# Inverse roots by a power instruction, the last fold stage on TensorE, and a new instruction order in a gated state-space and FFN kernel

## The reference, cut to what matters

```python
xc  = causal_conv4(in_proj_w @ ctx) + conv_b;  u = silu(xc)          # 256 channels
dt, Bm, Cm = split(x_proj_w @ u);  delta = softplus(dt_proj_w @ dt + dt_proj_b)
state = state * exp(delta * A) + (delta * u) * Bm;  y = sum_n(state * Cm)   # A = -exp(A_log)
y = swapaxes((y + D * u) * silu(layernorm(x)), 1, 2)      # layernorm(x) stands as (channel, token) here
x2 = x + tanh(g_xattn) * y
t  = act_quant(layernorm(x2))                  # per token: round(x * 128 / absmax)
h  = silu(t @ Wg_ternary) * (t @ Wu_ternary)
h  = act_quant(fwht(h))                        # Walsh-Hadamard over 1024
out = x2 + tanh(g_ffn) * (h @ Wd_ternary)
```

## Time and profile before

| | |
|---|---|
| three runs | 218.87, 219.84, 220.48 us, median 219.84 |
| profiled execution | 220.84 us, of which the span of instructions is 218.4 |
| busy | PE 195.1, DVE 185.9, ACT 170.4, POOL 106.7 us |
| first scan starts | 32.47 us |
| last `times_C` ends | 181.15 us |
| last instruction on DVE | 215.70 us |

### The profile page before, as it was taken

How to read it: one execution, slowest core, us unless ns; L and a number is a source line. 1 busy time by engine, 2 the same in 40 slices (tenths; PEclk the granted TensorE clock), 3 DMA queues, 4 the chain that set the end, 5 groups by cost and what they waited for, 6 DMA issues and landing times.

```text
span 218.4 us, 3808 instructions
## 1 busy us (share of the span) xinstructions
PE 195.1 (89%) x1296; PEld 160.7 (74%) x1296; DVE 185.9 (85%) x290; ACT 170.4 (78%) x298; POOL 106.7 (49%) x143
## 2 busy tenths in 40 slices
PE   2849997999999999999999999999899997669883
PEld 1638985898797888868889797888687676534761
DVE  1860709899989999999999999999999996879983
ACT  1357989999899998779997988899877812794473
POOL 1003080269805347935999992299940399600000
PEclk9967999999999999999999999999999999996998
DMA  5895000000000000000000000000000000000001
GB/s 139 236 358 193 3 2 2 0 0 3 0 0 3 0 0 6 0 0 0 5 0 0 3 0 0 27 2 24 3 0 0 2 27 24 0 0 3 24 24 48
DMA packets 8147, 6.33 MB, mean 29 GB/s; under 512 B 2202, under 2 KB 7874, under 8 KB 8130
## 3 DMA queue, kind: packets, MB, share of 16 engines
q1 hardware_dynamic: 6610, 6.01, 8.4%
q10 hardware_dynamic: 1520, 0.10, 0.5%
HBM read 5.05 MB, written 1.05 MB: 28 GB/s over the span
## 4 chain that ended last, share of the span: by engine, by line
PE 41%; POOL 7%; ACT 6%; DVE 5%; issue 2%; DVEq 0%; POOLq 0%; ACTq 0%
PE PY L477 8%; PE UP L414 7%; PE BC L414 6%; PE GP L596 5%; POOL wnat L1529 3%; POOL wnat L1530 3%; PE GP L627 2%; PE GP L611 2%; PE BC L461 2%; PE UP L649 1%; PE UP L668 1%; ACT ctxs L1200 1%; DVE state L1642 1%; DVE wnat L1828 1%; ACT wq L1239 1%
## 5 line engine op out<-in xcount | busy, mean ns | idle before, releaser
L1067 ACT ACTIVATE decay<-delta,zero_c,aneg 128x255 f32<-128x255 f32 x128 | 65.8, 590 | 0.2
L1642 DVE TENSOR_TENSOR_SCAN state<-decay,BC 128x512 f32<-128x512 f32 x32 | 38.8, 1212 | 8.3 <-ACT decay L1067 6.3
L1642 DVE TENSOR_TENSOR_SCAN state<-decay,UP 128x512 f32<-128x512 f32 x32 | 38.5, 1204 | 0.4 <-issue 0.2
L1725 DVE TENSOR_TENSOR prod<-state,BC 128x1024 f32<-128x1024 f32 x32 | 38.4, 1199 | 0.5 <-PE BC L461 0.5
L414 PE MATMUL BC<-diagB,duT 128*128 128x256 f32 x128 | 33.9, 387 | 1.0 <-DVE state L1642 1.0
L414 PE MATMUL UP<-diagB,duT 128*128 128x256 f32 x128 | 33.5, 385 | 1.1 <-DVE state L1642 1.1
L1529 POOL TENSOR_TENSOR wnat<-wnat 128x512 f32<-128x512 f32 x18 | 22.9, 1273 | 22.4 <-DVE wnat L1769 21.5
L477 PE MATMUL PY<-id,prod 128*128 128x128 f32 x256 | 32.8, 273 | 0.1
L477 PEld LDWEIGHTS PY<-id,prod 128*128 128x128 f32 x256 | 29.1, 141 | 2.3 <-DVE prod L1725 0.3
L1463 POOL TENSOR_SCALAR_AFFINE_SELECT diagB<-BT 128x1024 f32<-128x1024 f32 x16 | 17.3, 1090 | 22.1 <-ACT BT L1078 15.4
L414 PEld LDWEIGHTS UP<-diagB,duT 128*128 128x128 f32 x128 | 22.9, 190 | 6.2 <-issue 3.3
(11 more groups left out here) (254 smaller groups left out, 392.5 us busy)
## 6 DMA issues: line engine op xcount, KB each, us to landing
xs<-in_x_dram SPq DMA_DIRECT2D x1, 1024.0 KB, 8.6
wnat<-in_L_ffn_w_gate_dram SPq DMA_DIRECT2D x1, 1024.0 KB, 11.9
wnat<-in_L_ffn_w_up_dram SPq DMA_DIRECT2D x1, 1024.0 KB, 13.9
wnat<-in_L_ffn_w_down_dram SPq DMA_DIRECT2D x1, 1024.0 KB, 12.7
out_dram<-ot SPq DMA_DIRECT2D x8, 128.0 KB, 1.7
ctxs<-in_ctx_dram SPq DMA_DIRECT2D x1, 384.0 KB, 4.2
ctxs<-in_ctx_dram SPq DMA_DIRECT2D x1, 128.0 KB, 2.7
inw<-n_L_xattn_in_proj_w_dram SPq DMA_DIRECT2D x1, 128.0 KB, 2.8
```

What stands on the lines that cost most here:

```text
L1067: last = nc.scalar.activation(decay[:, m % RING, h, n, 1:L], delta[:, b % 2, h, 1:L], ACT.Exp, bias=zero_c[:], scale=aneg[:, h, NB * j + n ...
L1642: nc.vector.tensor_tensor_scan(state[:, g % STATES, h].rearrange("p n l -> p (n l)"), decay[:, g % RING, h].rearrange("p n l -> p (n l)"), ...
L1725: nc.vector.tensor_tensor(prod[:, g % RING].rearrange("p h n l -> p h (n l)"), state[:, g % STATES].rearrange("p h n l -> p h (n l)"), PC. ...
```

## The change

1. **Roots.** The first norm's inverse roots come from POOL: `first_rstd` there computes -mean, var + eps, (var + eps) ** -0.5 by a `tensor_tensor` with `ALU.pow` over 128x8, and the product. It stands ahead of `diagonals(0,0)`. ACT's Ln and Exp and DVE's four small instructions and two copies go. `second_rstd(f)` on POOL has one add, one power (128x2) and two small products, in place of ACT's `rstd2` and eight small POOL instructions. `last_rstd(c)` on POOL (add, power, product, 128x1) replaces ACT's Ln and Exp and DVE's `last_second_rstd(c)`; both calls stand after POOL's last `fold_tile(2,1,2)`.
2. **Table loads.** With no Ln and Exp in the tail, one `for_exp` and one `for_silu` go: `decays(31,*)` now come ahead of the Silu of batch 2, and the Silu set stays to the end.
3. **Last fold stage on PE.** `last_fold(t)` has two stages. The third is done by `last_inter_T` in PSUM: for each pair of blocks (a, a+1) it transposes a and accumulates the transpose of a+1, or a product with the negated identity (`nid`, made by POOL's `negate_id`). The halves hold other blocks (`last_block`).
4. **Loads.** The two gates move from ACT's queue to SP's, behind the Hadamard matrix and ahead of D; `alog` has its own semaphore and is issued earlier; `dtb` is issued ahead of x. `tanh_gates` moves behind the first `for_silu` after `decays(1,0)`; `gate_out(0)` waits for it.
5. **Order.** All four lists are rearranged.

```diff
+            def first_rstd():                                   # POOL
+                pool.wait_ge(dve_stat1, 1)
+                link_first.begin(pool, 0)
+                nc.gpsimd.tensor_scalar(nm1[:], mv1[:, :, 0], -1.0, 1.0, ALU.mult, ALU.mult)
+                link_first(nc.gpsimd.tensor_scalar(ve1[:], mv1[:, :, 1], LN_EPS, 0.0, ALU.add, ALU.add))
+                link_first(nc.gpsimd.tensor_tensor(r1[:], ve1[:], mhalf[:], ALU.pow))
+                nc.gpsimd.tensor_tensor(mr1[:], nm1[:], r1[:], ALU.mult).then_inc(pool_r1, 1)
             def second_rstd(f):
...
+                link(nc.gpsimd.tensor_scalar(ve2[:], mv2[:, :, 1], LN_EPS, 0.0, ALU.add, ALU.add))
+                link(nc.gpsimd.tensor_tensor(rn2[:], ve2[:], mhalf[:, 0:LC], ALU.pow))
                 for c in range(LC):
...
+            def last_rstd(c):
+                link = last_r_link[c].begin(pool, 0)
+                pool.wait_ge(last_stat, c + 1)
+                pool.wait_ge(act_xn, B - 1)
+                col = slice(c, c + 1)
+                link(nc.gpsimd.tensor_scalar(ve2[:, col], mv2[:, c, 1:2], LN_EPS, 0.0, ALU.add, ALU.add))
+                link(nc.gpsimd.tensor_tensor(rn2[:, col], ve2[:, col], mhalf[:, col], ALU.pow))
+                nc.gpsimd.tensor_scalar(mr2[:, col], mv2[:, c, 0:1], rn2[:, col], -1.0, ALU.mult, ALU.mult).then_inc(last_rn, 1)
...
             def last_inter_T(t, i):
-                pe.wait_ge(last_folded, 4 * t + 3 + i)
+                pe.wait_ge(last_folded, 3 * t + 2 + i)
...
-                for j in range(NI // 2):
-                    a = 2 * j + i
-                    last = nc.tensor.transpose(last_half(GP, i)[:, P * j:P * (j + 1)], fold[:, t, P * a:P * (a + 1)], id32[:])
+                for g in range(2):
+                    for k in range(2):
+                        dst = last_half(GP, i)[:, P * (2 * g + k):P * (2 * g + k + 1)]
+                        a = last_block(i, 2 * g)
+                        one, other = (inter[:, t, P * b:P * (b + 1)] for b in (a, a + 1))
+                        nc.tensor.matmul(dst, one, id32[:], is_transpose=True, start=True, stop=False)
+                        if k == 0:
+                            last = nc.tensor.matmul(dst, other, id32[:], is_transpose=True, start=False, stop=True)
+                        else:
+                            last = nc.tensor.matmul(dst, other, nid[:], start=False, stop=True)
...
+            for i, g in enumerate((g_xattn, g_ffn)):            # SP, after had, before dskip
+                sp.dma_start(gates[:, i:i + 1], g.partition_broadcast(P)).then_inc(ld_gate, 16)
```

More of the change, by code:

```diff
@@ L171, in gated_ssm_ffn @@
         bank6, bank7 = UP[:, 0:512], UP[:, 512:1024]
-        mean1, ve1, nt1 = (UP[:, 8 * i:8 * (i + 1)] for i in range(3))
         wgT = wT[:, 0].rearrange("p (h i) -> p h i", h=HALF)
@@ L814, in _ @@
             C_rows(7)
+            accumulate(4)
             drive_rows(9, 0)
-            accumulate(6)
-            weight_T(1)
-            drive_rows(9, 1)
-            C_rows(8)
-            weight_T(2)
-            dt_proj(2)
+            weight_T(2)
+            accumulate(5)
+            drive_rows(9, 1)
+            dt_proj(2)
+            C_rows(8)
+            accumulate(6)
+            drive_rows(10, 0)
             accumulate(7)
-            drive_rows(10, 0)
+            gate_T(1)
@@ L850, in _ @@
             C_rows(13)
             drive_rows(15, 0)
-            gate(0, 1)
+            up(0, 1)
             drive_rows(15, 1)
+            accumulate(11)
+            C_rows(14)
             accumulate(12)
-            C_rows(14)
-            up(0, 0)
             drive_rows(16, 0)
+            C_rows(15)
             drive_rows(16, 1)
-            C_rows(15)
             accumulate(13)
-            x_dbl(3)
             drive_rows(17, 0)
+            dt_proj(3)
             drive_rows(17, 1)
+            inter_T(0, 0)
@@ L888, in _ @@
-            hadamard_mm(0, 1)
-            down(0, 0)
-            accumulate(18)
-            tokens_T(1)
             drive_rows(22, 0)
-            drive_rows(22, 1)
-            accumulate(19)
+            du_T(3)
             gate(1, 0)
             C_rows(21)
+            drive_rows(22, 1)
+            gate(1, 1)
             drive_rows(23, 0)
-            du_T(3)
-            gate(1, 1)
+            gate_T(3)
+            q2_T(0, 1)
+            up(1, 0)
             drive_rows(23, 1)
+            drive_rows(24, 0)
@@ L901, in _ @@
+            C_rows(22)
+            down(0, 1)
             accumulate(20)
[L902 to L904 removed]
             drive_rows(24, 1)
[L906 to L908 removed]
             C_rows(23)
@@ L1033, in exp_A @@
                 act.wait_ge(consts, 1)
-                act.wait_ge(ld_gate, 16 * 3)
-                nc.scalar.activation(aneg[:], alog[:], ACT.Exp, bias=zero_c[:]).then_inc(act_gate, 1)
+                act.wait_ge(ld_A, 16)
+                nc.scalar.activation(aneg[:], alog[:], ACT.Exp, bias=zero_c[:]).then_inc(act_A, 1)
             def inw_out():
@@ L1211, in q2_out_early @@
                                ).then_inc(act_q2T, 1)
-            def last_rstd(c):
-                link = last_r_link[c].begin(act, 0)
-                act.wait_ge(last_stat, c + 1)
-                link(nc.scalar.activation(ln2[:, c:c + 1], mv2[:, c, 1:2], ACT.Ln, bias=eps_c[:]))
-                nc.scalar.activation(r2[:, c:c + 1], ln2[:, c:c + 1], ACT.Exp, bias=zero_c[:], scale=-0.5).then_inc(last_r, 1)
-                link.end()
             def last_norm(c):
@@ L1294, in _ @@
             for_exp()
+            dt_rows(1)
+            decays(1, 1)
+            copy_BT(1)
             decays(2, 0)
             decays(2, 1)
-            dt_rows(1)
-            copy_BT(1)
+            high_pieces(1)
             decays(3, 0)
-            high_pieces(1)
             decays(3, 1)
@@ L1303, in _ @@
             decays(4, 0)
+            softplus(1)
             decays(4, 1)
-            softplus(1)
-            gate_out(0)
             decays(5, 0)
             decays(5, 1)
+            gate_out(0)
+            weight_abs(1)
             weight_abs(2)
@@ L1823, in last_fold @@
                 dve.wait_ge(last_mul, 2 * (t + 1))
-                for i in range(FOLDS):
+                for i in range(FOLDS - 1):
                     src, dst = ((inter, fold), (fold, inter))[i % 2]
@@ L1922, in _ @@
             scan(0, 0)
-            first_rstd()
             scan(0, 1)
@@ L1979, in _ @@
             scan(14, 1)
+            gate_times_up(0, 0)
             times_C(13)
@@ L2046, in _ @@
             scan(29, 1)
+            gate_times_up(2, 0)
             times_C(28)
+            gate_times_up(2, 1)
             scan(30, 0)
-            gate_times_up(2, 0)
             scan(30, 1)
+            result(1, 0)
             times_C(29)
-            result(1, 0)
             scan(31, 0)
@@ L2055, in _ @@
             times_C(30)
-            gate_times_up(2, 1)
+            result(1, 1)
             times_C(31)
-            result(1, 1)
             last_residual()
@@ L2072, in _ @@
             last_gate_times_up(0, 1)
+            last_fold(0)
             round_down(2, 1)
-            last_fold(0)
             last_gate_times_up(1, 0)
+            result(2, 0)
             last_gate_times_up(1, 1)
-            result(2, 0)
             last_fold(1)
```

527 lines of the change are left out of this document (240 added, 287 removed).

## The result

The changed kernel takes **212.25 us** (median of 4 runs, 211.92 to 212.83) against 219.97 (218.87 to 220.48) for the kernel before on the same chip: ratio 0.966, 95% interval 0.961 to 0.970. Forecast were 209.7, with a range of 205.5 to 215.

What follows compares the result with a forecast made beforehand. DVE and PE were taken to share the bound in the scans, so only their start and the tail count: 220.84 - 6.5 (start) - 4.65 (tail), with 0 for the scans, gave 209.7 us, range 205.5 to 215.

Steps and rivals of the forecast that it cites:

- forecast case of 205.5 to 212: Whole kernel: the prediction's main case, a time of 205.5 to 212 us, given a chance of 0.64.
- Start: Up to scan(6,0): late gates, earlier silu_u(0) and a warm PE save 6.5 us, bounds 4.5 to 8.
- I carry the shift at 0: Scans: the stretch only slides earlier and its length changes by 0 us, bounds -1.5 and +2.
- Tail: After the last times_C: roots, last fold and table load together save 4.65 us, bounds 2.5 to 6.
- T + 4.5: Tail: POOL's folds end 4.5 us after T, the end of times_C(31), instead of 7.1.
- 1.75 + 0.4: Tail: DVE loses eight Newton instructions, 1.75 us, and removing ACT's table load gives 0.4 us.
- a forecast of 2.5: Tail: moving the third fold stage to PE saves 1.3 us on last_fold(0) and net 1.2 on last_fold(1).
- a sign against the forecast: Tail: the forecast would be wrong if DVE waits for norms there.
- That the start's gain isn't carried: Rival, first batch: ACT becomes the bound, DVE and PE idle 2 us more; start worth 3 to 4 us; chance 0.16.
- PE cold: Rival, start: a wait drops PE's clock, costing 3 to 4 us, 1 more in the tail; 213 to 215; chance 0.07.
- The stall on `up(2,0)`: Rival, tail: gate_times_up(2,0) stalls, POOL's folds hide the gain, tail gives 2 us, 212.5 us; chance 0.04.
- The slow power: Rival, roots on POOL: a slow power per column makes the kernel slower than before from 1.3 us; chance 0.05.

Runs made afterwards that it cites:

- run 1: The kernel before with only the gate loads moved to SP's queue, alog on its own semaphore and tanh moved later: 215.16 us, ratio 0.982.
- run 2: The changed kernel with the gate loads back in ACT's queue ahead of alog and tanh early again: 218.86 us, ratio 0.996.
- run 8: Also written a_start: the changed kernel with PE's and ACT's lists at the start in another order: 213.38 us, ratio 0.971.
- run 10: The changed kernel with all four lists in the old order through the middle, new order in start and tail: 214.27 us, ratio 0.977.
- run 6: The changed kernel with the three power instructions on POOL replaced by products, so the roots are left out: 211.2 us, ratio 0.963.
- run 7: The changed kernel with diagonals(3,2) moved from between two folds of batch 1 to behind token_factors(2): 211.75 us, ratio 0.965.
- run 4: The changed kernel with the last batch's roots by Ln, Exp and Newton again, with their two table loads: 215.3 us, ratio 0.985.
- run 11: The changed kernel with the four lists in the old order from the third drive_rows up to scan(24,0) only: 214.43 us, ratio 0.976.

## Why the prediction was right, and where not

The time is right by its range (205.5 to 215), not by its middle: 212.25 is 2.5 us above the 209.7 and just outside the forecast case of 205.5 to 212. An error in the scans of 3.65 us was partly made good by one in the start, and that is luck.

**Start: right in mechanism, 1.1 us too small** (7.6 for 6.5, within the bounds). The causes are as put: a load that tanh need not wait for (runs 1, 2), PE warm (run 2 shows the price of a cold one), and ACT's list (run 8). From `decays(0,0)` to the end of `decays(6,0)` I counted 27.4 us; the trace has 19.12 to 46.54 = 27.4. What I mis-sized lies ahead of it. I had the convolution stay at 8.36; it began at 7.41, and `silu_u(0)` ran at 9.87 instead of 11.5. PE is at work from 1.58 us now, but so it is in `a_start`, where the convolution began at 8.32: the 0.95 us belong to this execution and aren't shown to be the fillers' doing. ACT, which I had with nothing in hand at `scan(6,0)`, was done with `decays(6,0)` 0.5 us ahead of it (46.54 and 47.07). The stall ahead of the second step is 1.95 us and waits for PE (`drive_rows(1,0)` behind `x_dbl(1)`), where I had 3 us waiting for `decays(1,1)` ahead of `scan(1,1)`; run 8 shows that it costs nothing at `scan(6,0)`.

**Scans: wrong.** The step that failed is "I carry the shift at 0", with bounds -1.5 and +2. The stretch lost 3.65 us; 0.46 of it is `result(1,1)`, which moved into it, and that leaves 3.2. DVE's idle time went from 2.46 to 5.07 us, more than the bound of +2 allowed for. What the runs attribute:
- up to `scan(24,0)` 1.1 us, which the old order gives back whole (run 10), with the powers in place. In the new order 0.5 of them go too when the powers become products (run 6).
- behind it 2.1 us, of which 0.94 is the stall at `scan(27,0)`: POOL's folds, with the diagonals and the root between them (runs 6, 7). Taking out the diagonals shrinks it by 0.73 us, the power's price by 0.56.
- the last 1.15 us behind `scan(24,0)` no run attributes. The traces name part: DVE idles 2.22 us there (before 0.46), beside the 0.94 also 0.48 ahead of `times_C(31)`, for `C_rows(31)` in PE's list, and 0.25 ahead of `gate_times_up(2,0)` (before 0.15). Neither was tested. A kernel with the new parts and the old order through to the last scan was not tried; by the kernel before it would have the folds of batch 2 end some 3 us later (7.1 us behind the last `times_C` instead of 3.8), with the roots on POOL behind them.

I had costed the power on the tail only and called the scans' roots a saving of small instructions. I had not walked POOL's list through batch 1's folds, where two steps of 1.08 and 1.6 us were put in a chain that PE waits for.

**Tail: right, with one term wrong in each direction.** 4.25 us for 4.65. From the residual to `gate_times_up(0,0)` it took 11.93 us before and 9.58 after: 2.35 for a forecast of 1.75 + 0.4. From there to the last result 20.46 and 18.42: 2.04 for a forecast of 2.5. The power took 0.58 us on one column where I took 0.5, and POOL's folds ended at T + 3.8 for T + 4.5. DVE does wait for the norm, 0.86 us ahead of `last_round(0)`, which I had named as a sign against the forecast; it cost less than the Newton instructions had. Undoing the parts within the new order costs more (3.16 and 2.64) than they brought, presumably since that order was made around them; the load was worth 1.28 us there and not 0.4 (run 4). PE's half with six transposes and two products took 1.1 us, as worked out.

**Rivals.** That the start's gain isn't carried, 0.16: half of it came. Not the half of ACT, since the gain reached `scan(6,0)`; but its condition that DVE idle 2 us more in the new order did (2.6 us), start and scans together gave 3.95 us where it said 3 to 4, and 212.25 us is just short of its 212.5. I had its size right and its weight too low. PE cold: not in this kernel's start, but one hole of 2 us away from it in the scans (runs 2, 8, 11). The stall on `up(2,0)`: 0.25 us, too small to matter. The slow power: 0.58 us, far below the 1.3 from which it would have decided. By the three terms the profiled execution would be 220.84 - 7.6 + 3.65 - 4.25 = 212.6 us; it was 211.92, since the time around the span fell from 2.4 to 1.7 us. The forecast of 209.7 was 3.65 too low in the scans and 0.4 in the tail, and 1.1 too high in the start.
